# First attention of a two-block transformer: the query and key projections copied twice by ScalarE and added by GpSimd, where VectorE built them from PSUM

## The chip, the cores and the metric

The kernel runs on one core of a Trainium2 chip. The metric is the device time of one execution in microseconds (us), smaller is better. TensorE does the matrix products and writes PSUM; VectorE and ScalarE read PSUM and SBUF; GpSimd reads SBUF alone; SyncE issues the DMAs of this stage.

## The reference

The input `x` is 4 sequences of 1024 tokens with 128 features. Six sublayers follow one another, each on a normalised input and with a residual: a mixture of experts, causal attention, the same mixture again, a feed-forward layer in FP4, a second attention, the FP4 layer again. The change lies in the first attention alone:

```
def _L0_attn_ref(x, Wqkv, Wout, bout):
    qkv = x @ Wqkv.T                                # 16 heads of 8
    q, k, v = map(merge_heads, jnp.split(qkv, 3, axis=-1))
    dots = jnp.einsum('bhid,bhjd->bhij', q, k) * dh ** (-0.5)
    dots = jnp.where(causal_mask, -jnp.inf, dots)
    attn = jax.nn.softmax(dots, axis=-1)
    out = jnp.einsum('bhij,bhjd->bhid', attn, v)
    return out @ Wout.T + bout
```

## The kernel before

The first attention is one function, `attention0_stage`. The work is cut into 16 groups: 4 sequences by 4 groups of 4 heads. A head takes 32 partitions, of which 8 hold the value, 8 the part that rounding to the matmul type (`F32R`) loses, and two carry the row maximum.

Per group there are three kinds of work on the score matrix, in 20 units each (`NE` = `NM` = 20), numbered by `e`:

- MAX(e), function `max_unit`: TensorE writes scores for queries by keys (L1712, on the diagonal also L1716) into one of three PSUM buffers `pS` of 1024 columns. VectorE reduces it to maxima (L1979, `z_parts`).
- EXP(e), function `exp_unit`: TensorE writes the transposed scores, less the maximum (L1736), into a `pS` buffer. ScalarE takes the exponential into `Pr` (L1894). GpSimd zeroes what lies behind the diagonal in 8 blocks a group (`select`, L2083).
- `values` (L1750): TensorE multiplies `Pr` with V into `pO`, after several EXP units; ScalarE copies the result to `oT` (L1881).

While group G has its EXP units, group G+1 has its MAX units, and group G+2 its projections. TensorE's program in `main(G)` goes through e = 0 to 19, and at each e does MAX(G+1, e), then whatever falls due at this e (turns, a projection, `values`), then EXP(G, e). The three `pS` buffers go round over this order, so MAX(e) takes the buffer of EXP(e-2), and EXP(e) that of MAX(e-1):

```
                    if u >= 3:
                        before, g, k = USES[u - 3]
                        need(pe, *((maxed, NM * g + k + 1) if before == MAXIMUM else (exp_done, NE * g + k + 1)))
```

That is, MAX(e) on TensorE waits until ScalarE is done with the exponential of EXP(e-2), and EXP(e) waits until VectorE is done with the reduction of MAX(e-1).

A group's queries and keys come in four projections (`project`, L1662, three matmuls of 512 columns each), at e = 3, 9, 13 and 17 (`AT_PROJECT`), in the order query low half, key low half, key high half, query high half. All write one PSUM bank, `pX`, which also serves the turning of maxima (`turn_maximum`, at e = 2 and 15) and of outputs (`turn_output`, at e = 5 and 11). A projection is kept in two steps. ScalarE, ahead of its exponential of the same e, writes the rounded value to `high` (`keep_high`, L1871); VectorE, ahead of its reduction of the next e, multiplies `high` with a column of factors (0, 1 or -1 by row), adds the projection from PSUM, and writes `Q` or `QK` (`split`, L1968). `split_done` counts the latter. TensorE waits for it before it writes `pX` again and before the group's MAX(0); SyncE waits for it before it copies keys into `KM` (`spread_keys`, L1605), after which, in its queue, come the maxima into `QM` (`spread_maxima`, L1623), and queries (`spread_queries`, L1616).

There are such projections within `main` for groups 2 to 15, that is in `main(0)` to `main(13)`: 56 of them in 14 groups. The first eight are done ahead of it. `main(14)` has MAX and EXP units but no projections, `main(15)` only EXP units.

Of the kernel before, what the change touches and what calls it, by code (L numbers as in the profile page):

```python
# [4 lines left out]
F32 = mybir.dt.float32  # L5
# [5 lines left out]
P = 128  # L11
# [56 lines left out]
def need(engine, sem, n):  # L68

    if not isinstance(n, int) or n > 0:  # L70
        engine.wait_ge(sem, n)
# [1412 lines left out]
def attention0_stage(nc, C, name, Wt):  # L1484
# [9 lines left out]
    with Scope(nc, name) as s:  # L1494
# [10 lines left out]
        QK = [s.sb(f"QK{u}", [P, SEQ0], F32R) for u in range(RING)]  # L1505
        KM = [s.sb(f"KM{u}", [P, 2, SEQ0], F32R) for u in range(2)]
        QM = [s.sb(f"QM{u}", [P, 2, SEQ0 // 2], F32R) for u in range(2)]
        high = s.sb("high", [P, 512], F32R)
        Pr = [s.sb(f"Pr{u}", [P, 4, 512]) for u in range(4)]
        parts, m = s.sb("parts", [P, KT, KT, 4]), s.sb("m", [P, KT, 4])  # L1510
        mw = s.sb("mw", [P, KT, 4, 32], F32R)
# [82 lines left out]
        with nc.Block() as block:  # L1594
# [58 lines left out]
            def _(pe):  # L1653
# [112 lines left out]
                def main(G):  # L1766
                    more, further, first = G + 1 < NG, G + 2 < NG, G % 4 == 0 and G > 0
                    for e in range(NE):
                        if more:
                            max_unit(G + 1, e)  # L1770
                        if e == AT_M1:
                            need(pe, split_done, min(4 * (G + 2), 4 * NG))
                            need(pe, m_kept, 2 * G + 1)
                            turn_maximum(G, 1)
                        if e == AT_PROJECT[0] and further:
                            need(pe, m_kept, 2 * G + 2)
                            project(G + 2, Q_LOW)
                        if e == AT_O1 and G > 0:
                            need(pe, *((split_done, 4 * (G + 2) + 1) if further else (m_kept, 2 * G + 2)))
                            turn_output(G - 1, 1)  # L1780
                        if e in AT_FIN and first:
                            need(pe, o_normed, 2 * G)
                            need(pe, fin_kept, 2 * (G // 4 - 1) + AT_FIN.index(e))
                            turn_batch(G // 4 - 1, AT_FIN.index(e))
                        if e == AT_PROJECT[1] and further:
                            need(pe, split_done, 4 * (G + 2) + 1)
                            need(pe, o_normed, 2 * G)
                            if first:
                                need(pe, fin_kept, 2 * (G // 4))
                            project(G + 2, K_LOW)  # L1790
                        if e == AT_O0:
                            if further:
                                need(pe, split_done, 4 * (G + 2) + 2)
                            else:
                                need(pe, o_normed, 2 * G)
                            turn_output(G, 0)
                        if e == AT_PROJECT[2] and further:
                            need(pe, o_normed, 2 * G + 1)
                            project(G + 2, K_HIGH)
                        if e == AT_M0 and more:  # L1800
                            if further:
                                need(pe, split_done, 4 * (G + 2) + 3)
                            else:
                                need(pe, o_normed, 2 * G + 1)
                            turn_maximum(G + 1, 0)
                        if e == AT_PROJECT[3] and further:
                            need(pe, m_kept, 2 * G + 3)
                            project(G + 2, Q_HIGH)
                        for j in range(NJ):
                            if AT_V[j] == e:  # L1810
                                values(G, j)
                            if AT_V[j] - NE == e and G > 0:
                                values(G - 1, j)
                        exp_unit(G, e)
# [49 lines left out]
            def _(act):  # L1864
                a = nc.scalar

                def keep_high(G, i, k):

                    need(act, proj_done, 4 * G + k + 1)
                    need(act, split_done, 4 * G + k)  # L1870
                    a.activation(high[:, :], bank(G, i), ACT.Identity, bias=rows[:, 1 - i // 2:2 - i // 2]).then_inc(high_done, 1)  # L1871

                def keep_maximum(G, half):
                    need(act, m_turned, 2 * G + half + 1)
                    need(act, q_masked[half], 128 * G)
                    a.activation(mT[half][:, :], pX[:, :], ACT.Copy).then_inc(m_kept, 1)
# [20 lines left out]
                def main(G):  # L1897
                    more, further, first = G + 1 < NG, G + 2 < NG, G % 4 == 0 and G > 0
                    for e in range(NE):
                        if e == AT_M1:  # L1900
                            keep_maximum(G, 1)
                        if e == AT_TAKE[1] and G > 0:
                            keep_output(G - 1, 1)
                        if e == AT_TAKE[0]:
                            keep_output(G, 0)
                        if e in AT_FIN and first:
                            keep_batch(G // 4 - 1, AT_FIN.index(e))
                        if e == AT_M0 and more:
                            keep_maximum(G + 1, 0)
                        if e in AT_PROJECT and further:  # L1910
                            keep_high(G + 2, ORDER[AT_PROJECT.index(e)], AT_PROJECT.index(e))
                        exponentials(G, e)

                def high_rows(w):
# [41 lines left out]
            def _(dve):  # L1956
                v = nc.vector

                def split(G, i, k):

                    need(dve, high_done, 4 * G + k + 1)

                    dst = Q[G % 2] if i // 2 else QK[G % RING]
                    if i // 2:
                        need(dve, st_ready, NE * (G - 2) + (NE0 if i % 2 else 0) + 1 if G >= 2 else 0)
                    else:
                        need(dve, st_ready, NE * (G - RING + 1))
                    v.scalar_tensor_tensor(dst[:, (i % 2) * 512:(i % 2) * 512 + 512], high[:, :].bitcast(F32),  # L1968
                                           rows[:, 3 - i // 2:4 - i // 2], bank(G, i), ALU.mult, ALU.add).then_inc(split_done, 1)
# [34 lines left out]
                                    r.unsqueeze(3).to_broadcast([P, 4, 4, DH0]), ALU.mult).then_inc(o_normed, 1)  # L2004

                def main(G):
                    more, further = G + 1 < NG, G + 2 < NG
                    for n in range(NM + 1):
                        if n == AT_MAX and more:
                            maximum(G + 1, 0)  # L2010
                        if n == AT_O1 + 1 and G > 0:
                            output(G - 1, 1)
                        for k in range(4):
                            if n == AT_PROJECT[k] + 1 and further:
                                split(G + 2, ORDER[k], k)
                        if n == AT_O0 + 1:
                            output(G, 0)
                        if n < NM and more:
                            max_unit(G + 1, n)
                    if more:  # L2020
                        maximum(G + 1, 1)
# [52 lines left out]
            @block.gpsimd  # L2074
            def _(pool):
                g_ = nc.gpsimd

                def select(G, j, c):

                    need(pool, exp_done, NE * G + FIRST_OF[j] + 1)  # L2080
                    blk = Pr[j % 4][:, :, c * P:(c + 1) * P]

                    g_.affine_select(blk, blk, [[0, 4], [1, P]], ALU.is_ge, 0.0, base=0, channel_multiplier=-1).then_inc(selected, 1)  # L2083

                g_.memset(KM[0][:, 0, :].bitcast(F32), 0.0).then_inc(zeroed, 1)

                pool.wait_ge(xn_ready, NT)
                g_.memset(parts[:, :, :, :], -BIG).then_inc(ready, 1)
                g_.memset(V[:, :, :, DH0:DH0 + 1], 1.0).then_inc(ones_set, 1)
                g_.memset(mw[:, :, :, :].bitcast(F32), 0.0).then_inc(ready, 1)  # L2090
                for buf in (QM[0], KM[1], QM[1]):
                    g_.memset(buf[:, :, :].bitcast(F32), 0.0).then_inc(zeroed, 1)
                xt = X[:, :].rearrange("p (t f) -> p t f", f=D)
                pool.wait_ge(bo_loaded, 16)
                pool.wait_ge(xn_ready, NT)
                g_.tensor_tensor(xt, xt, bo.unsqueeze(1).to_broadcast([P, NT, D]), ALU.add).then_inc(biased, 1)
                for G in range(NG):
                    for c in range(4):
                        select(G, c, c)
                    for c in range(4):  # L2100
                        select(G, 8 + c, c)


def build(nc, d, out):
# [110 lines left out]
```

## Time and profile before

| | |
|---|---|
| median of 3 runs | 1815.1 us (1807.4 to 1815.26) |
| profiled execution, its own time | 1809.93 us |
| its span | 1808.0 us |
| stretch of this attention's groups | about 345 to 845 us |
| granted TensorE clock, mean | 0.922 |

The profile's page gives busy time by engine and the costliest groups of instructions. The trace behind it is asked for stretches: a timeline row is a start, a duration, an engine, a line of the kernel, the tensors (written <- read) and a count where like instructions ran on end; a bracket gives the idle time ahead of it on its engine and whose work ended it.

### The profile page before, as it was taken

The numbers are of one execution on the slowest core, as the hardware profiler recorded it, in microseconds if no ns is written. First come the engines' busy times: TensorE is split into PE (matmuls) and PEld (weight loads), VectorE is DVE, ScalarE is ACT, GpSimd is POOL, SyncE is SP. The second block draws the span as 40 slices with busy tenths as digits, with TensorE's granted clock in tenths as the row PEclk, the third lists the DMA queues.
The fourth block names the chain that finished last, engine by engine and source line by source line (L and its number), as shares of the span: only waits on it lengthen the run. The fifth ranks groups of instructions, "written<-read, shape, count | busy, mean of one in ns | idle before, by whom it ended". The sixth has DMA issues, their size and how long they took to land. (4 is left out here: it accounts for less than half of the span.)

```text
span 1808.0 us, 35347 instructions
## 1 busy us (share of the span) xinstructions
PE 1524.2 (84%) x12511; PEld 1008.8 (56%) x12511; DVE 1199.7 (66%) x2260; ACT 971.2 (54%) x1727; POOL 690.6 (38%) x1145
## 2 busy tenths in 40 slices
PE   6999966999999999998799896456888889888874
PEld 5568853544443444434666785234666667676653
DVE  6635558588888888883754565656566777766434
ACT  3324432377777777775343442323677667667641
POOL 0687743011111111111088764342244454453432
PEclk9999988599999999998699998677999999999987
DMA  7122521011111111110513242100000000000000
GB/s 257 35 78 75 148 84 32 20 35 27 27 39 27 36 30 34 27 26 7 208 42 92 85 131 79 52 0 1 2 2 2 5 8 5 5 8 9 7 4 13
DMA packets 49469, 81.52 MB, mean 45 GB/s; under 512 B 10868, under 2 KB 34868, under 8 KB 48628
## 3 DMA queue, kind: packets, MB, share of 16 engines
q1 hardware_dynamic: 40212, 60.50, 11.5%
q0 software_dynamic: 9088, 18.76, 3.1%
q8 instruction: 107, 1.75, 0.4%
q14 instruction: 62, 0.51, 0.1%
HBM read 43.18 MB, written 31.22 MB: 41 GB/s over the span
## 5 line engine op out<-in xcount | busy, mean ns | idle before, releaser
L1979 DVE TENSOR_REDUCE z_parts<-z_pS 128x8 f32<-128x1024 f32 (+1 forms) x320 | 350.5, 1115 | 51.4 <-PE z_pS L1712 33.4
L1894 ACT ACTIVATE z_Pr<-z_pS 128x1024 f32<-128x1024 f32 (+1 forms) x320 | 297.5, 940 | 121.2 <-PE z_pS L1736 120.6
L2083 POOL TENSOR_SCALAR_AFFINE_SELECT z_Pr<-z_Pr 128x512 f32<-128x512 f32 x128 | 80.8, 637 | 445.5 <-ACT z_Pr L1894 445.5
L356 POOL DMA_INDIRECT slot_results<-m_yq,m_xq x156 | 153.9, 987 | 75.6 <-ACT m_yq L561 45.3
L332 POOL DMA_INDIRECT slot_rows<-m_XN,m_dest x128 | 129.9, 1015 | 93.7 <-DVE m_dest L650 58.3
L1750 PE MATMUL z_pO<-z_Pr,z_V 128*9 128x512 f32 (+3 forms) x1536 | 160.2, 489 | 3.1 <-ACT z_oT L1881 1.6
L1736 PE MATMUL z_pS<-z_QM,z_QK 64*128 64x512 f32 (+1 forms) x640 | 150.4, 470 | 1.4 <-DVE z_parts L1979 0.2
L1736 PEld LDWEIGHTS z_pS<-z_QM,z_QK 64*128 64x128 f32 x640 | 59.7, 185 | 155.4 <-issue 111.6
L1712 PE MATMUL z_pS<-z_KM,z_Q 64*128 64x512 f32 (+1 forms) x640 | 133.2, 414 | 15.1 <-ACT z_Pr L1894 14.7
L974 PE MATMUL f_gup<-s_wguT,f_xT 128*128 128x352 f32 x234 | 97.7, 501 | 34.2 <-DVE f_src L1281 19.0
L705 DVE TENSOR_TENSOR m_h<-m_sg,m_gu 128x512 f32<-128x512 f32 x78 | 53.7, 688 | 90.9 <-ACT m_sg L553 90.8
L1156 ACT ACTIVATE f_vb<-f_p 64x256 f32<-64x256 f32 x256 | 97.0, 379 | 31.0 <-PE f_p L949 28.2
L1281 DVE TENSOR_TENSOR f_src<-f_sg,f_gup 128x176 f32<-128x176 f32 x117 | 38.4, 328 | 104.9 <-ACT f_sg L1125 104.3
L553 ACT ACTIVATE m_sg<-m_gu 128x512 f32<-128x512 f32 x78 | 46.6, 598 | 101.5 <-PE m_gu L450 101.5
L1125 ACT ACTIVATE f_sg<-f_gup 128x176 f32<-128x176 f32 x117 | 37.6, 321 | 107.1 <-PE f_gup L974 106.7
L1712 PEld LDWEIGHTS z_pS<-z_KM,z_Q 64*128 64x128 f32 x640 | 62.4, 191 | 40.5 <-ACT z_Pr L1894 28.2
L597 DVE TENSOR_TENSOR m_h<-m_sg,m_gu 128x512 f32<-128x512 f32 x64 | 44.0, 687 | 60.7 <-PE m_gu L374 54.2
L1444 POOL TENSOR_TENSOR f_pm<-f_Pn,k_mask 128x512 f32<-128x512 f32 x64 | 82.7, 1307 | 1.3 <-DVE f_Pn L1316 1.3
L1420 POOL TENSOR_TENSOR f_q<-f_y,f_neg 128x256 f32<-128x256 f32 x32 | 19.9, 623 | 163.6 <-issue 161.8
L1412 POOL TENSOR_SCALAR f_neg<-f_sc 128x60 f32<-128x60 f32 (+2 forms) x36 | 12.7, 353 | 181.2 <-DVE f_sc L1260 166.0
L529 ACT ACTIVATE m_sg<-m_gu 128x512 f32<-128x512 f32 x64 | 38.1, 599 | 78.0 <-PE m_gu L370 76.1
L450 PE MATMUL m_gu<-s_wh,m_xqh 128*128 x156 | 71.1, 456 | 8.4 <-issue 6.4
(296 smaller groups left out, 3852.3 us busy)
## 6 DMA issues: line engine op xcount, KB each, us to landing
slot_rows<-in_c_pad SPq DMA_DIRECT2D x2, 5070.0 KB, 24.9
m_xq<-slot_rows SPq DMA_DIRECT2D x38, 260.0 KB, 4.3
z_KM<-z_QK SPq DMA_DIRECT2D x60, 128.0 KB, 2.4
z_QM<-z_Q SPq DMA_DIRECT2D x128, 48.0 KB
m_raw<-in_gu SPq DMA_DIRECT2D x2, 2048.0 KB, 9.1
m_XN<-slot_results SPq DMA_DIRECT2D x8, 512.0 KB, 4.1
m_raw<-slot_results SPq DMA_DIRECT2D x8, 512.0 KB, 5.5
slot_results<-m_yq,m_xq POOLq DMA_INDIRECT x156
```

The source lines that it names most:

```text
L332: g_.indirect_dma_start(xs_dram, bass.IndirectOffsetOnAxis(dest[:, k, t:t + 1], 0), XN[:, t, 2 - XO[k]:2 - XO[k] + ROW], None).then_inc(se ...
L356: g_.indirect_dma_start(y_dram, bass.IndirectOffsetOnAxis(xq[q % RING][:, j % QT, TAG[list_of(j)]:TAG[list_of(j)] + 1].bitcast(I32), 0), y ...
L450: last = mm(gu[r % 2][:, u, :], xv[q % 2][:, c], wt[:, bass.ds(es[u] * GU, GU)], start=a, stop=b)
L974: mm(bank[:, 0:INNER], xT[:, j * P:(j + 1) * P], wguT[:, c, :, :].rearrange("p a k -> p (a k)"), start=True, stop=True).then_inc(gated, 1)
L1156: last = a_.activation(vb[j % 2][a * 64:(a + 1) * 64, g * 256:(g + 1) * 256].rearrange("p (k d) -> p k d", k=4), heads, ACT.Copy)
L1444: g_.tensor_tensor(pm[j % 2][:, :, :, :], Pn[:, h0:h0 + 8, :].unsqueeze(3).to_broadcast([P, 8, SEQ1, PER]), mask16[:, :].unsqueeze(1).unsq ...
L1712: last = mm(b[:, 2 * pair:2 * pair + 2, 0:width * P], Q[G % 2][r, qt * P:(qt + 1) * P], KM[G % 2][r, :, kb * P:(kb + width) * P], start=Tr ...
L1736: last = mm(b[:, 2 * pair:2 * pair + 2, 0:width * P], QK[G % RING][r, kt * P:(kt + 1) * P], QM[half][r, :, q * P:(q + width) * P], start=T ...
L1750: last = mm(pO[32 * h:32 * h + DH0 + 1, lo:512], V[:, (G // 4) * KT + kt, 4 * (G % 4) + h, :], Pr[j % 4][:, h, lo:512], start=(kt == 0), s ...
L1894: a.activation(Pr[j % 4][:, :, q * P:(q + width) * P], heads(G, EXPONENTIAL, e)[:, :, 0:width * P], ACT.Exp, scale=DH0 ** -0.5).then_inc(e ...
L1979: v.tensor_reduce(parts[:, qt, kb:kb + width, :].rearrange("p t h -> p h t"), b.rearrange("p h (t k) -> p h t k", k=P), AX.X, ALU.max).the ...
L2083: g_.affine_select(blk, blk, [[0, 4], [1, P]], ALU.is_ge, 0.0, base=0, channel_multiplier=-1).then_inc(selected, 1)
```

## The change

ScalarE's `keep_high` of the 56 projections in `main` becomes `keep_both`: `high` is now the rounded value of the projection times the factor plus the bias, both from columns of `rows`, and a second instruction copies the projection unrounded to a new SBUF tile `whole`. GpSimd adds the two into `Q` or `QK`. VectorE no longer does it. TensorE's waits before it writes `pX` again ask for `high_done`, which both copies together raise once, in place of `split_done`. GpSimd's program now has the adds between its selects, in the order of e. The first eight projections stay as they were.

```diff
-        high = s.sb("high", [P, 512], F32R)
+        high, whole = s.sb("high", [P, 512], F32R), s.sb("whole", [P, 512])
...
                         if e == AT_M1:
-                            need(pe, split_done, min(4 * (G + 2), 4 * NG))
+                            need(pe, high_done, min(4 * (G + 2), 4 * NG))
...
                         if e == AT_O1 and G > 0:
-                            need(pe, *((split_done, 4 * (G + 2) + 1) if further else (m_kept, 2 * G + 2)))
+                            need(pe, *((high_done, 4 * (G + 2) + 1) if further else (m_kept, 2 * G + 2)))
...
                         if e == AT_PROJECT[1] and further:
-                            need(pe, split_done, 4 * (G + 2) + 1)
+                            need(pe, high_done, 4 * (G + 2) + 1)
...
                         if e == AT_O0:
                             if further:
-                                need(pe, split_done, 4 * (G + 2) + 2)
+                                need(pe, high_done, 4 * (G + 2) + 2)
...
                         if e == AT_M0 and more:
                             if further:
-                                need(pe, split_done, 4 * (G + 2) + 3)
+                                need(pe, high_done, 4 * (G + 2) + 3)
...
+                def keep_both(G, i, k):
+
+                    need(act, proj_done, 4 * G + k + 1)
+                    need(act, split_done, 4 * G + k)
+                    a.activation(high[:, :], pX[:, :], ACT.Identity, bias=rows[:, 1 - i // 2:2 - i // 2], scale=rows[:, 3 - i // 2:4 - i // 2])
+                    a.activation(whole[:, :], pX[:, :], ACT.Copy).then_inc(high_done, 1)
...
                         if e in AT_PROJECT and further:
-                            keep_high(G + 2, ORDER[AT_PROJECT.index(e)], AT_PROJECT.index(e))
+                            keep_both(G + 2, ORDER[AT_PROJECT.index(e)], AT_PROJECT.index(e))
                         exponentials(G, e)
...
-                        for k in range(4):
-                            if n == AT_PROJECT[k] + 1 and further:
-                                split(G + 2, ORDER[k], k)
...
+                def split(G, i, k):
+
+
+                    pool.wait_ge(high_done, 4 * G + k + 1)
+                    need(pool, st_ready, NE * (G - 2) + (NE0 if i % 2 else 0) + 1 if i // 2 else NE * (G - RING + 1))
+                    dst = Q[G % 2] if i // 2 else QK[G % RING]
+                    g_.tensor_tensor(dst[:, (i % 2) * 512:(i % 2) * 512 + 512], high[:, :].bitcast(F32), whole[:, :], ALU.add).then_inc(split_done, 1)
...
-                    for c in range(4):
-                        select(G, c, c)
-                    for c in range(4):
-                        select(G, 8 + c, c)
+                    for e in range(NE):
+                        if e in AT_PROJECT and G + 2 < NG:
+                            split(G + 2, ORDER[AT_PROJECT.index(e)], AT_PROJECT.index(e))
+                        j = EU[e][0]
+                        if e == FIRST_OF[j] and not 4 <= j < 8:
+                            select(G, j, j % 4)
```

ScalarE, `main(1)`, e = 1 to 4, around the projection at e = 3. Before:

```order
L1894 ACTIVATE z_Pr0<-z_pS1 128x4x256
L1876 ACTIVATE z_mT1<-z_pX 128x512
L1894 ACTIVATE z_Pr1<-z_pS0 128x4x128
L1881 ACTIVATE z_oT<-z_pO 128x512
L1871 ACTIVATE z_high<-z_pX,k_rows 128x512
L1894 ACTIVATE z_Pr1<-z_pS2 128x4x256
L1894 ACTIVATE z_Pr2<-z_pS1 128x4x256
```

The same place of the changed kernel (its lines have other numbers from here on; L1901 are the exponentials):

```order
L1901 ACTIVATE z_Pr0<-z_pS1 128x4x256
L1883 ACTIVATE z_mT1<-z_pX 128x512
L1901 ACTIVATE z_Pr1<-z_pS0 128x4x128
L1888 ACTIVATE z_oT<-z_pO 128x512
L1877 ACTIVATE z_high<-z_pX,k_rows 128x512
L1878 ACTIVATE z_whole<-z_pX 128x512
L1901 ACTIVATE z_Pr1<-z_pS2 128x4x256
L1901 ACTIVATE z_Pr2<-z_pS1 128x4x256
```

One copy more stands between the rounded value and the exponential of e = 3; it is so at each of the four projections.

VectorE, the same stretch of `main(1)`, reductions of MAX(3) to MAX(5), then the output of the group before. Before:

```order
L1979 TENSOR_REDUCE z_parts<-z_pS1 128x4
L1968 SCALAR_TENSOR_TENSOR z_Q1<-z_high,k_rows,z_pX 128x512
L1979 TENSOR_REDUCE z_parts<-z_pS0 128x4x2
L1979 TENSOR_REDUCE z_parts<-z_pS2 128x4x2
L1998 RECIPROCAL z_rec<-z_pX 128x16
L2003 TENSOR_TENSOR z_at<-z_pX,z_rec 128x4x32
```

Changed:

```order
L1986 TENSOR_REDUCE z_parts<-z_pS1 128x4
L1986 TENSOR_REDUCE z_parts<-z_pS0 128x4x2
L1986 TENSOR_REDUCE z_parts<-z_pS2 128x4x2
L2005 RECIPROCAL z_rec<-z_pX 128x16
L2010 TENSOR_TENSOR z_at<-z_pX,z_rec 128x4x32
```

The one instruction on `high` is gone, nothing else moved.

GpSimd, one group of the changed kernel, where before eight selects stood on end (the adds are L2095; x2 are those of e = 9 and 13):

```order
L2087 AFFINE_SELECT z_Pr0<-z_Pr0 128x4x128
L2087 AFFINE_SELECT z_Pr1<-z_Pr1 128x4x128
L2095 TENSOR_TENSOR z_Q1<-z_high,z_whole 128x512
L2087 AFFINE_SELECT z_Pr2<-z_Pr2 128x4x128
L2087 AFFINE_SELECT z_Pr3<-z_Pr3 128x4x128
L2095 TENSOR_TENSOR z_QK0<-z_high,z_whole 128x512 x2
L2087 AFFINE_SELECT z_Pr0<-z_Pr0 128x4x128
L2087 AFFINE_SELECT z_Pr1<-z_Pr1 128x4x128
L2095 TENSOR_TENSOR z_Q1<-z_high,z_whole 128x512
L2087 AFFINE_SELECT z_Pr2<-z_Pr2 128x4x128
L2087 AFFINE_SELECT z_Pr3<-z_Pr3 128x4x128
```

TensorE's and SyncE's instructions keep their order; only the semaphores that TensorE waits on before it writes `pX` change.

## Rows read from the trace of the kernel before

**Rows 1.** The page: busy time, share and instructions of each engine.

```profile
PE 1524.2 (84%) x12511; PEld 1008.8 (56%) x12511; DVE 1199.7 (66%) x2260; ACT 971.2 (54%) x1727; POOL 690.6 (38%) x1145
```

**Rows 2.** Busy time in 31 us of the groups: PE, PEld, DVE, ACT, POOL, clock, DMA.

```profile
562.00:593.00 31.00, 29.93 (x224) 12.71 (x220) 26.35 (x35) 22.42 (x29) 5.05 (x8) 1.00 0.13 31
```

**Rows 3.** Timeline of ScalarE over one group: start, duration, instruction, idle time before.

```profile
571.69 0.59 ACT L1876 ACTIVATE z_mT<-z_pX 128x512 fp32r<-128x512 f32 x1
...
573.97 1.93 ACT L1894 ACTIVATE z_Pr<-z_pS 128x1024 f32<-128x1024 f32 x2
...
582.57 0.59 ACT L1881 ACTIVATE z_oT<-z_pO 128x512 f32<-128x512 f32 x1
583.04 0.69 ACT L1871 ACTIVATE z_high<-z_pX,k_rows 128x512 fp32r<-128x512 f32 x1
583.61 1.04 ACT L1894 ACTIVATE z_Pr<-z_pS 128x1024 f32<-128x1024 f32 x1
...
589.77 1.02 ACT L1894 ACTIVATE z_Pr<-z_pS 128x1024 f32<-128x1024 f32 x1
...
592.18 0.59 ACT L1876 ACTIVATE z_mT<-z_pX 128x512 fp32r<-128x512 f32 x1
...
595.30 0.69 ACT L1871 ACTIVATE z_high<-z_pX,k_rows 128x512 fp32r<-128x512 f32 x1 [0.52 <-PE z_pX L1662]
595.88 1.02 ACT L1894 ACTIVATE z_Pr<-z_pS 128x1024 f32<-128x1024 f32 x1
597.37 1.61 ACT L1894 ACTIVATE z_Pr<-z_pS 128x1024 f32<-128x1024 f32 x2 [0.47 <-PE z_pS L1736]
...
602.94 0.59 ACT L1876 ACTIVATE z_mT<-z_pX 128x512 fp32r<-128x512 f32 x1
```

**Rows 4.** Timeline of TensorE's matmuls in the same group.

```profile
573.84 0.40 PE L1736 MATMUL z_pS<-z_QM,z_QK 64*128 64x512 f32 x2
575.04 0.50 PE L1712 MATMUL z_pS<-z_KM,z_Q 64*128 64x512 f32 x2 [0.80 <-ACT z_Pr L1894]
...
584.70 0.50 PE L1712 MATMUL z_pS<-z_KM,z_Q 64*128 64x512 f32 x2
...
591.06 0.28 PE L1712 MATMUL z_pS<-z_KM,z_Q 64*128 64x256 f32 x2
...
597.16 0.39 PE L1712 MATMUL z_pS<-z_KM,z_Q 64*128 64x512 f32 x2
...
597.96 0.38 PE L1736 MATMUL z_pS<-z_QM,z_QK 64*128 64x256 f32 x2
598.53 0.39 PE L1712 MATMUL z_pS<-z_KM,z_Q 64*128 64x256 f32 x2 [0.20 <-ACT z_Pr L1894]
```

**Rows 5.** VectorE: the splits of the 28 query halves, by form; then its timeline.

```profile
L1968 DVE SCALAR_TENSOR_TENSOR z_Q<-z_high,k_rows,z_pX 128x512 fp32r<-128x512 f32 x28 | 20.9, 748 | 16.2 <-ACT z_high L1871 14.9 <-PE z_pS L1736 1.3
```

```profile
596.68 2.46 DVE L1979 TENSOR_REDUCE z_parts<-z_pS 128x8 f32<-128x1024 f32 x2
```

**Rows 6.** ScalarE's two copies of turned maxima in `main(14)`, which has no projections.

```profile
792.15 0.59 ACT L1876 ACTIVATE z_mT<-z_pX 128x512 fp32r<-128x512 f32 x1
811.55 0.59 ACT L1876 ACTIVATE z_mT<-z_pX 128x512 fp32r<-128x512 f32 x1
```

**Rows 7.** Groups by form: ScalarE's copies, one with a bias column; a GpSimd tensor_tensor.

```profile
L1871 ACT ACTIVATE z_high<-z_pX,k_rows 128x512 fp32r<-128x512 f32 x56 | 38.6, 689 | 10.7 <-PE z_pX L1662 8.7
L1876 ACT ACTIVATE z_mT<-z_pX 128x512 fp32r<-128x512 f32 x30 | 17.8, 593 | 0.8 <-PE z_pX L1724 0.8
L1431 POOL TENSOR_TENSOR f_wl<-f_raw,f_wh 128x512 fp32r<-128x512 f32 x2 | 2.5, 1269 | 0.0
```

**Rows 8.** GpSimd's selects of e = 18 and 19; SyncE's four key copies.

```profile
598.46 1.23 POOL L2083 TENSOR_SCALAR_AFFINE_SELECT z_Pr<-z_Pr 128x512 f32<-128x512 f32 x2 [2.98 <-ACT z_Pr L1894]
```

```profile
590.68 4.05 SPq L1605 DMA_DIRECT2D z_KM<-z_QK  x4
```

```profile
z_KM<-z_QK SPq DMA_DIRECT2D x60, 128.0 KB, 2.4
```

More of the change, by code:

```diff
@@ L2006, in main @@
                 def main(G):
-                    more, further = G + 1 < NG, G + 2 < NG
+                    more = G + 1 < NG
                     for n in range(NM + 1):
```

## Prediction

> **What bounds the kernel now.** The page comes first: TensorE is busy 84% of the span, VectorE 66%, ScalarE 54%, GpSimd 38% [rows 1]. These are averages over six sublayers, and the change touches one, so the second view is the stretch in which its groups run. There the core repeats itself: in 31 us TensorE is busy 29.93, VectorE 26.35, ScalarE 22.42 and GpSimd 5.05, with the clock granted in full [rows 2]. ScalarE's copy of a turned maximum at e = 2 comes at 571.69 and again at 602.94, so a group takes 31.25 us [rows 3]. By busy time TensorE is the limit, VectorE second, ScalarE third. But busy shares don't tell what a change on the second or third is worth; for that one must see which waits TensorE has, since its program is in order and goes on end between them.
>
> The third view is TensorE's timeline over one group, read for matmuls that start right when another engine's work ends. Five places matter:
>
> - MAX(5) at 575.04, with 0.80 us idle ahead of it [rows 4]. MAX(5) needs the exponential of EXP(3); ScalarE's two exponentials from 573.97 took 1.93 in all, one alone takes 1.02, so that of EXP(3) ended at 574.99, 0.05 ahead of the matmul [rows 3, 4].
> - MAX(11) at 584.70. The exponential of EXP(9), 583.61 plus 1.04, ended at 584.65, again 0.05 ahead [rows 3, 4]. There is no idle time ahead of it in the row, but no reserve either.
> - MAX(15) at 591.06. The exponential of EXP(13) ended at 590.79: a reserve of 0.27 [rows 3, 4].
> - MAX(19) at 597.16. That of EXP(17) ended at 596.90: a reserve of 0.26 [rows 3, 4].
> - EXP(19) at 597.96 and the next group's MAX(0) at 598.53. EXP(19) needs the reduction of MAX(18), which ended at about 596.68 plus 1.23, 597.91; this is the one place of the group where VectorE holds TensorE. I estimate the hold at 0.15 us: from MAX(19) to EXP(19) are 0.80 us, and MAX(19) with its diagonal, two rows of matmuls, accounts for some 0.65 of them. MAX(0) needs the exponential of EXP(18), 597.37 plus 1.02, 598.39 [rows 3 to 5].
>
> So MAX(5), MAX(11), MAX(15) and MAX(19) each wait, or nearly so, for the exponential that stands right behind a projection's copy in ScalarE's program. That makes ScalarE's order at the four projections, not VectorE's load, what the change acts upon.
>
> **VectorE's part, removed.** 56 splits of 0.748 us go, 3.0 us in each of 14 groups, and with them the wait ahead of each for `high`, 14.9 over the 28 query halves, 0.53 each [rows 5]: 5.1 us a group or 72 us in all. On the path only the 0.15 us at EXP(19) answers to it, 2.1 us over 14 groups, and the wait for ScalarE at the next MAX(0) right behind would take even this. I credit 0.
>
> **ScalarE's part, added.** The second copy has the shape of the copy of maxima, 0.593 [rows 7]. What counts is how far it pushes the next start: from `oT` at 582.57 (0.59 long) to `high` at 583.04 is 0.47, so such instructions overlap, and I take 0.48 [rows 3]. `high` now has a column as factor besides the column as bias. With the bias alone it is 0.689 against 0.593 without, so a column costs 0.096 [rows 7]; for the factor no row here reads PSUM with both, so it lies between 0 and 0.10, and I take 0.09, by the nearest row. Together 0.57 us a projection.
>
> The Trainium skill, in "ScalarE: Activation LUTs", section "What ACT_TABLE_LOAD costs", says that each per-partition pointer operand adds about 93 ns, factor and bias alike. The row for the bias agrees (96 ns); by the page as an estimate the sum stays as it is, by a free factor it would be 4 us less.
>
> Where does 0.57 go?
>
> - e = 3: the exponential of EXP(3) already holds MAX(5). All of it is lost: 0.57.
> - e = 9: MAX(11) has no reserve: 0.57.
> - e = 13: the exponential ends at 591.36, plus 0.05 is 591.41 against 591.06: 0.35.
> - e = 17: MAX(19) moves to 597.52, 0.36 late, EXP(19) behind it to about 598.25. But MAX(0) can't start before the exponential of EXP(18), whose matmuls lie ahead of MAX(19) and haven't moved, and which ScalarE, free at 595.88 + 0.57 + 0.91 = 597.36, can start at 597.37 as before. MAX(0) stays at 598.53: 0.
>
> Between these points TensorE goes on end, so what is lost at one isn't won back at the next. Sum: 1.49 us a group, times 14 is 20.9 us. Bounds: with a free factor 0.48 + 0.48 + 0.26 is 1.22, or 17 us; with nothing absorbed at e = 17 and 0.1 us more at the two new waits for restarting the matmul stream it is about 2.05, or 29 us.
>
> **GpSimd's part, added.** 56 adds of 128x512 fp32 into fp32r. A tensor_tensor of just this form takes 1.269 [rows 7]. GpSimd idles 26 of 31 us [rows 2], so the load, 5.1 us a group, is covered. Three users wait behind it. The selects: at e = 17 `high` starts at 595.30, both copies end at about 596.56, the add at 597.9; the next select came at 598.46, bound by its exponential [rows 3, 8]: 0.5 us to spare. The next group's MAX(0) needs all four adds: 597.9 against 598.53 [rows 4], 0.6 to spare. SyncE's key copies started at 590.68, right behind the split; the add of e = 13 ends 1.1 us later, at 591.8. They took 4.05 here to be issued and 2.4 to land [rows 8], so 598.3, just ahead of MAX(0), which itself moves by the 1.49. All at 0. If this cover were gone, each 0.1 us would cost 1.4 us in all.
>
> **TensorE's waits for `pX`** now end with ScalarE's two copies and not with the split. No turn waits for them now, so nothing is won.
>
> **Sum.** 1809.9 + 20.9 = 1830.8 us for an execution like the profiled one. This one lies 5.2 us under the median of the three runs, 1815.1; put on the median the sum is 1836.0. I forecast 1833, between the two.
>
> **Rivals.**
>
> *VectorE sets the pace after all* (faster). For it: 85% busy here, and 72 us taken from it. `main(14)` shows the most that can come: without projections it needs 811.55 - 792.15 = 19.40 us from e = 2 to e = 15, where the normal group needs 592.18 - 571.69 = 20.49 [rows 3, 6]. Three projections gone from all engines give 1.09, four some 1.45, over 14 groups 20 us. If half of this came through VectorE and ScalarE's copy cost nothing: 1800 us. It decides if TensorE waited for reductions by over 0.65 us a group more than for exponentials; I find 0.15. Chance 0.12.
>
> *ScalarE's second copy is hidden* (same). ScalarE idles 8.6 us of 31. It would need the exponentials behind projections not to be what MAX waits for; at MAX(5) and MAX(11) the 0.05 us gaps say they are. 1810 to 1815 us. Chance 0.10.
>
> *The add comes too late* (slower still). If GpSimd needs over 1.9 us from copy to result at e = 17, or the key copies land late, the next MAX(0) waits. At 2.5 us it is 0.6 a group more, 8 us: 1841. The measured 1.269 speaks against it. The Trainium skill, in "GPSIMD Engine Reference", section "Performance versus the Vector engine", puts a two-input add at 1.96 times VectorE's time. On the split's 0.748 that is an estimate of 1.47 us, still inside the 1.9; the row is shorter. Chance 0.13.
>
> *The forecast*, 0.65, own range 1825 to 1844.
>
> **How the numbers follow.** The range 1811 to 1846 takes the forecast's cases, most of the late add and the upper part of the hidden copy; the faster case and the tails are left out, some 0.2. Half a percent, 9 us, is about what a measurement of this kernel can tell from no change. Faster: 0.12. Same: the hidden copy and the forecast's lowest tail, 0.12. Slower: 0.76.
>
> **What would show it.** The period between copies of turned maxima at 32.7 us in place of 31.25; MAX(5) again right behind the exponential of EXP(3), with 1.4 us idle ahead of it in place of 0.80; MAX(11) with a wait of 0.6; VectorE's idle time up by 3 us a group and more; `high` at 0.78 us, `whole` at 0.59, the add at 1.27 with no one behind it. A period under 31.25 would prove me wrong on VectorE, one over 33.3 on the add or the keys.

## The result and the profile after

| | before | changed |
|---|---|---|
| median of 6 runs | 1807.94 us (1802.26 to 1815.26) | 1827.24 us (1819.34 to 1832.1) |
| span of the profiled execution | 1808.0 us | 1823.5 us |
| period of a group | 31.25 us | 32.75 us |

The changed kernel takes 1.0100 times the time before, 95% interval 1.0068 to 1.0132: 19.3 us slower by the medians, where 20.9 was forecast. The median before came down by 7 us with three more runs, so the absolute 1833 was some 6 us too high; the difference is what the sum was about.

The view by form over the groups (count | busy us, mean ns | idle us before and its releasers) shows the instructions that the change is made of; their counterparts in the kernel before stand in [rows 5] and [rows 7].

```profile
L1877 ACT ACTIVATE z_high<-z_pX,k_rows 128x512 fp32r<-128x512 f32 x56 | 43.6, 779 | 10.9 <-PE z_pX L1662 8.8
L2095 POOL TENSOR_TENSOR z_QK<-z_high,z_whole 128x512 fp32r<-128x512 f32 x28 | 35.7, 1274 | 155.3 <-ACT z_whole L1878 155.3
L2095 POOL TENSOR_TENSOR z_Q<-z_high,z_whole 128x512 fp32r<-128x512 f32 x28 | 35.6, 1271 | 33.9 <-ACT z_whole L1878 33.9
L1878 ACT ACTIVATE z_whole<-z_pX 128x512 f32<-128x512 f32 x56 | 33.1, 591 | 0.0
```

`high` went from 689 to 779 ns with the factor column, `whole` takes 591, the add 1271 to 1274. Busy times in 33 us of the groups (PE, PEld, DVE, ACT, POOL), against [rows 2] in 31:

```profile
445.00:478.00 33.00, 30.77 (x224) 12.82 (x222) 24.43 (x31) 25.02 (x33) 10.38 (x13) 1.00 0.13 30
```

TensorE has 2.2 us idle in 33 where it had 1.1 in 31. ScalarE's timeline of one group, as in [rows 3]:

```profile
443.58 0.59 ACT L1883 ACTIVATE z_mT<-z_pX 128x512 fp32r<-128x512 f32 x1
...
445.28 0.78 ACT L1877 ACTIVATE z_high<-z_pX,k_rows 128x512 fp32r<-128x512 f32 x1
445.96 0.59 ACT L1878 ACTIVATE z_whole<-z_pX 128x512 f32<-128x512 f32 x1
446.44 1.94 ACT L1901 ACTIVATE z_Pr<-z_pS 128x1024 f32<-128x1024 f32 x2
...
476.36 0.59 ACT L1883 ACTIVATE z_mT<-z_pX 128x512 fp32r<-128x512 f32 x1
```

And TensorE's, as in [rows 4]:

```profile
447.51 0.50 PE L1712 MATMUL z_pS<-z_KM,z_Q 64*128 64x512 f32 x2 [1.38 <-ACT z_Pr L1901]
...
457.76 0.50 PE L1712 MATMUL z_pS<-z_KM,z_Q 64*128 64x512 f32 x2 [0.48 <-ACT z_Pr L1901]
...
464.50 0.38 PE L1712 MATMUL z_pS<-z_KM,z_Q 64*128 64x256 f32 x2 [0.17 <-ACT z_Pr L1901]
...
470.95 0.49 PE L1712 MATMUL z_pS<-z_KM,z_Q 64*128 64x512 f32 x2 [0.20 <-ACT z_Pr L1901]
...
471.96 0.38 PE L1712 MATMUL z_pS<-z_KM,z_Q 64*128 64x256 f32 x2
```

The reader should see the new brackets: MAX(5) waits 1.38 us where it waited 0.80, and MAX(11), MAX(15) and MAX(19), which had no bracket, have one. Counted from the group's first copy of turned maxima (571.69 before, 443.58 now), the five matmuls stand as follows:

| | before | now | later by | added here |
|---|---|---|---|---|
| MAX(5) | 3.35 | 3.93 | 0.58 | 0.58 |
| MAX(11) | 13.01 | 14.18 | 1.17 | 0.59 |
| MAX(15) | 19.37 | 20.92 | 1.55 | 0.38 |
| MAX(19) | 25.47 | 27.37 | 1.90 | 0.35 |
| next MAX(0) | 26.84 | 28.38 | 1.54 | -0.36 |

The forecast had 0.57, 0.57, 0.35, 0.36 and back to 1.49.

VectorE, for its part, gained idle time and nothing else. Its reductions in the stretch of the groups, wider form, in the views of the kernel before and of the changed one:

```profile
L1979 DVE TENSOR_REDUCE z_parts<-z_pS 128x8 f32<-128x1024 f32 x242 | 291.9, 1222 | 31.5 <-PE z_pS L1712 22.7 <-PE z_pS L1716 8.4
L1986 DVE TENSOR_REDUCE z_parts<-z_pS 128x8 f32<-128x1024 f32 x239 | 291.1, 1224 | 101.0 <-PE z_pS L1716 55.8 <-PE z_pS L1712 45.0
```

VectorE now waits 101 us for TensorE ahead of these reductions, where it waited 31.5 us.

### The profile page after: what moved, and what is told of

It reads as the page before. It is cut to its first block and busy times, and to the rows that moved or that the text cites. A ratio compares the mean times of both kernels' runs of the same rounds, so it can differ in the third digit from the quotient of the medians.

```text
span 1823.5 us, 35401 instructions
## 1 busy us (share of the span) xinstructions
PE 1520.8 (83%) x12509; PEld 1003.3 (55%) x12511; DVE 1165.5 (64%) x2204; ACT 999.5 (55%) x1783; POOL 759.5 (42%) x1201
## 5 line engine op out<-in xcount | busy, mean ns | idle before, releaser
L1901 ACT ACTIVATE z_Pr<-z_pS 128x1024 f32<-128x1024 f32 (+1 forms) x320 | 293.4, 942 | 109.9 <-PE z_pS L1736 109.5
L2095 POOL TENSOR_TENSOR z_QK<-z_high,z_whole 128x512 fp32r<-128x512 f32 x28 | 35.7, 1274 | 155.3 <-ACT z_whole L1878 155.3
```

The costliest lines, as they stand in the source:

```text
L1901: a.activation(Pr[j % 4][:, :, q * P:(q + width) * P], heads(G, EXPONENTIAL, e)[:, :, 0:width * P], ACT.Exp, scale=DH0 ** -0.5).then_inc(e ...
```

## The experiments

The experiments ran on three chips, each kernel beside the kernel before on the same chip, with 5 to 12 executions of a kernel and 16 to 30 of the kernel before. These chips ran the kernel before at 1838 to 1844 us, where it took 1808 above, so only ratios and the period of a group are compared. The period is the distance from one group's copy of turned maxima to the next group's, in the profiled execution. Groups 4, 8 and 12 also turn a sequence's result and take longer, most by 0.85 us; all periods given are those of the others. The kernel before has one profile, with the period 31.25; the changed kernel has two, on two chips, with the same period in both.

| kernel | period, us | time against before (95%) |
|---|---|---|
| before | 31.25 | 1 |
| changed | 32.76 | 1.0100 (1.0068 to 1.0132) |
| changed, on another chip | 32.76 | 1.0100 (1.0069 to 1.0131) |
| no second copy | 31.45 | 1.0028 (1.0001 to 1.0054) |
| before, plus a copy | 32.57 | 1.0109 (1.0085 to 1.0132) |
| double add | 33.43 | 1.0149 (1.0116 to 1.0183) |
| three copies | 34.70, some 36.25 | 1.0304 (1.0281 to 1.0327) |
| copy behind the exponential | 31.42 | 1.0025 (1.0005 to 1.0044) |
| both copies of e = 9 behind | 32.40 | 1.0070 (1.0045 to 1.0095) |
| changed, reordered | 30.81 | 0.9940 (0.9918 to 0.9962) |
| before, reordered | 31.82 | 1.0043 (1.0021 to 1.0066) |
| changed, reordered at e = 17 too | 30.56 | 0.9948 (0.9923 to 0.9973) |

My theory was that of the prediction: the loss is the time by which ScalarE's copies push back the exponential behind them, at the places where TensorE waits for it, and VectorE's relief is worth nothing. The rivals: GpSimd's adds or the later key copies are the loss; VectorE's relief is worth something and the copies cost more; ScalarE's total load counts, not its order.

**The second copy taken out.**

```diff
-                    a.activation(high[:, :], pX[:, :], ACT.Identity, bias=..., scale=...)
-                    a.activation(whole[:, :], pX[:, :], ACT.Copy).then_inc(high_done, 1)
+                    a.activation(high[:, :], pX[:, :], ACT.Identity, bias=..., scale=...).then_inc(high_done, 1)
...
+                g_.memset(whole[:, :], 0.0)
```

> The changed kernel without ScalarE's second copy: whole is set to zero once and GpSimd adds the constant, so the queries and keys of groups 2 to 15 lack their unrounded part and the output is not the reference's. VectorE still has no splits, GpSimd still has its adds. My theory (the copy ahead of the exponential is the whole loss, VectorE's relief is worth nothing): only the factor column of high is left, 0.09 us at e = 3 and at e = 9, swallowed at e = 13 and 17. Period 31.4 us against 31.25 before, time 2 to 3 us above the kernel before. Rival (VectorE's relief is worth something that the copy hides): a period clearly under 31.25, down to 30, and a time 5 to 15 us under the kernel before.

This kernel leaves out the unrounded part. The period is 31.45. Of the 1.51 us, 1.31 are gone with this one instruction, while the adds and the missing splits are still there. (The adds and the keys do come one copy earlier; whether they matter, the next two experiments test.) What is left, 0.20, is two times the 0.09 of the factor column, and no relief by VectorE shows. The time is 1.0028 of the kernel before, by the interval just above it.

**The kernel before with a copy added.**

```diff
                         if e in AT_PROJECT and further:
                             keep_high(G + 2, ORDER[AT_PROJECT.index(e)], AT_PROJECT.index(e))
+                            a.activation(whole[:, :], wh[:, 0:512].bitcast(F32), ACT.Copy)
                         exponentials(G, e)
```

> The kernel before, with one ScalarE copy more behind keep_high at each of the 56 projections (from SBUF into a tile that nobody reads). VectorE keeps its splits, nothing goes to GpSimd. My theory: 0.48 us at e = 3 and e = 9, 0.2 at e = 13, none at e = 17, so a period of 32.4 and 16 to 18 us above the kernel before, 3 to 5 below the changed one. Rival (the loss of the change is in GpSimd's adds or the later key copies): within 3 us of the kernel before. Rival (VectorE's relief did help in the changed kernel): clearly slower than the changed kernel.

```profile
L1912 ACT ACTIVATE z_whole<-s_wh 128x512 f32<-128x512 f32 x49 | 30.6, 625 | 0.0
```

That is the view by form of this kernel. With VectorE's splits in place and nothing on GpSimd the period is 32.57, 1.32 above before, so the copy alone makes nearly the whole loss. That is 0.17 above the 1.15 expected. The copy from SBUF takes 625 ns where the one from PSUM takes 591, and this difference is paid at three places, 0.10 in all; the rest is the 0.05 us from the exponential's end to MAX(15), which the 0.2 expected at e = 13 had left out. The changed kernel has 0.19 more. At e = 3, 9 and 13 its factor column pushes 0.09 and its copy 0.03 less than this one, 3 times 0.06 together, so the splits that it no longer has on VectorE were worth less than these views resolve. By time I had expected this kernel 3 to 5 us below the changed one; the two can't be told apart (1.0109 and 1.0100, intervals that overlap widely).

**Each add done twice.**

```diff
+                    g_.tensor_tensor(spare[:, :], high[:, :].bitcast(F32), whole[:, :], ALU.add)
                     g_.tensor_tensor(dst[:, (i % 2) * 512:(i % 2) * 512 + 512], high[:, :].bitcast(F32), whole[:, :], ALU.add).then_inc(split_done, 1)
```

> The changed kernel with each GpSimd add done twice, first into a spare tile: 2.5 us from copy to result in place of 1.27. My theory: the add was covered by 0.6 us only at e = 17; with the doubled one the next group's MAX(0) waits for it some 0.7 us, the key copies still land in time. Period about 33.4 us, 8 to 11 us above the changed kernel. Rival (the add was already on the path): 1.27 us a group or more, 18 us or more above. Rival (wide cover): nothing.

TensorE's weight loads of this kernel show the next group's MAX(0) behind GpSimd:

```profile
430.67 0.18 PEld L1713 LDWEIGHTS z_pS<-z_KM,z_Q 64*128 64x128 f32 x2 [0.73 <-POOL z_Q L2097]
...
464.10 0.19 PEld L1713 LDWEIGHTS z_pS<-z_KM,z_Q 64*128 64x128 f32 x2 [0.73 <-POOL z_Q L2097]
```

The period is 33.43, 0.67 above the changed kernel: of 1.27 us more a projection, 0.6 were covered, as worked out. The list of this kernel's waits names no DMA, so the keys, which come later by as much, held nothing up. The add is not on the path of the changed kernel, but more than 0.6 us of further work on GpSimd at e = 17 would put it there.

**A third copy.**

```diff
+                    a.activation(spare[:, :], pX[:, :], ACT.Copy)
                     a.activation(whole[:, :], pX[:, :], ACT.Copy).then_inc(high_done, 1)
```

> The changed kernel with a third ScalarE copy of each projection, into a spare tile, between high and whole. My theory: now there is no reserve left anywhere, so 0.48 us is lost at all four projections: period 32.75 + 1.9 = 34.7 us, 25 to 28 us above the changed kernel. Rival (the copies are partly hidden in ScalarE's idle time): 10 us or less.

Seven of the thirteen periods behind the first group are undisturbed and 34.7 (or 35.6 with a turned sequence), 1.94 above the changed kernel: with the reserves gone, all four places pay 0.48. That is as expected. But the time rose by 0.0204 of 1841, some 38 us, and not 27. Six periods are 1.55 us longer than their like, 9.3 us in all, and a table by stretches shows what goes with it. Its columns are the stretch, its length, the busy time of PE, PEld, DVE, ACT and POOL, then the granted clock, the DMA share and GB/s. First such a group, with MAX(5) at 408.93, then one without, with MAX(5) at 445.18:

```profile
404.00:409.00 5.00, 3.14 (x29) 1.82 (x28) 2.97 (x3) 4.95 (x9) 1.59 (x2) 1.00 0.08 18
409.00:410.00 1.00, 1.00 (x8) 0.69 (x8) 0.21 (x1) 0.79 (x1) 0.45 (x2) 1.00 0.00 0
410.00:411.00 1.00, 1.00 (x10) 0.12 (x8) 1.00 (x2) 0.00 (x0) 0.49 (x1) 0.64 0.00 0
411.00:412.00 1.00, 1.00 (x10) 0.16 (x2) 0.47 (x3) 0.00 (x0) 0.00 (x0) 0.50 0.00 0
412.00:413.00 1.00, 1.00 (x8) 0.47 (x12) 0.10 (x1) 0.53 (x1) 0.00 (x0) 0.50 0.00 0
413.00:414.00 1.00, 1.00 (x10) 0.03 (x2) 1.00 (x1) 0.06 (x1) 0.64 (x1) 0.65 0.07 18
...
440.00:445.00 5.00, 3.32 (x29) 1.99 (x27) 3.22 (x4) 4.95 (x9) 1.38 (x3) 1.00 0.05 13
445.00:446.00 1.00, 0.82 (x6) 0.56 (x7) 0.00 (x0) 1.00 (x2) 0.56 (x1) 1.00 0.00 0
446.00:447.00 1.00, 1.00 (x13) 0.32 (x10) 0.96 (x1) 0.04 (x1) 0.63 (x1) 1.00 0.06 16
```

In the first the granted clock was 0.50 of full from 411 to 413 and between the two in the slices on either side. Eight matmuls of `values`, 1.04 us long in the other group, took 1.79 there:

```profile
408.93 0.50 PE L1713 MATMUL z_pS<-z_KM,z_Q 64*128 64x512 f32 x2 [1.86 <-ACT z_Pr L1903]
...
410.12 1.79 PE L1751 MATMUL z_pO<-z_Pr,z_V 128*9 128x512 f32 x8
```

**The copy moved behind the exponential.** At e = 3, 9 and 13:

```diff
                     a.activation(high[:, :], pX[:, :], ACT.Identity, bias=..., scale=...)
+                    if e is not None:
+                        exponentials(G - 2, e)
                     a.activation(whole[:, :], pX[:, :], ACT.Copy).then_inc(high_done, 1)
...
-                            keep_both(G + 2, ORDER[AT_PROJECT.index(e)], AT_PROJECT.index(e))
-                        exponentials(G, e)
+                            keep_both(G + 2, ORDER[AT_PROJECT.index(e)], AT_PROJECT.index(e), e if e in (3, 9, 13) else None)
+                        if not (further and e in (3, 9, 13)):
+                            exponentials(G, e)
```

> The changed kernel, but at e = 3, 9 and 13 the copy to whole stands behind the exponential of the same e and not ahead of it; high stays ahead, e = 17 is as in the changed kernel. All the same instructions run. My theory: the exponentials that MAX(5), MAX(11) and MAX(15) wait for come 0.48 us earlier again, only the factor column's 0.09 us is lost at e = 3 and 9; the exponentials of e = 4, 10 and 14, now later, have that much reserve. Period 31.4 to 31.5 us, 2 to 5 us above the kernel before. Rival (ScalarE's total load is what costs): a period of 32.5 or more, as in the changed kernel.

```profile
402.38 0.78 ACT L1877 ACTIVATE z_high<-z_pX,k_rows 128x512 fp32r<-128x512 f32 x1
403.06 1.01 ACT L1903 ACTIVATE z_Pr<-z_pS 128x1024 f32<-128x1024 f32 x1
403.96 0.60 ACT L1880 ACTIVATE z_whole<-z_pX 128x512 f32<-128x512 f32 x1
404.44 1.03 ACT L1903 ACTIVATE z_Pr<-z_pS 128x1024 f32<-128x1024 f32 x1
```

The same instructions on the same engines, three pairs of them swapped, and the period is 31.42 where it was 32.76. ScalarE's load is not what costs; the place in its queue is. This is the plainest of the experiments.

**Both copies of e = 9 behind the exponential.**

```diff
-                        if e in AT_PROJECT and further:
+                        if e in AT_PROJECT and e != 9 and further:
                             keep_both(G + 2, ORDER[AT_PROJECT.index(e)], AT_PROJECT.index(e))
                         exponentials(G, e)
+                        if e == 9 and further:
+                            keep_both(G + 2, ORDER[AT_PROJECT.index(e)], AT_PROJECT.index(e))
```

> The changed kernel with both copies of the projection of e = 9 behind the exponential of EXP(9). My theory: MAX(11) waits no more, 0.57 us of the 1.5 come back and nothing else changes: period 32.2 us, 12 to 14 us above the kernel before. Rival (a loss at one place is made up at the next, so that repairing one doesn't help): period 32.6 or more.

The period is 32.40: 0.36 came back, not 0.57. The view of weight loads names what took the rest, the turn of outputs at e = 11, which writes `pX` and must now wait until ScalarE has read it:

```profile
416.25 0.42 PEld L1757 LDWEIGHTS z_pX<-k_ident,z_oT 128*128 128x128 f32 x4 [0.36 <-ACT z_whole L1878]
```

What I had not counted is that a copy moved back on ScalarE also frees `pX` later. Counted from the start of the projection's last matmul, `whole` ends at 3.04 us here and at 1.98 in the changed kernel. Where `whole` alone was moved, it ended at 2.89; TensorE came to the turn at 3.01 and did not wait.

**A new order for the changed kernel.** If order is what costs, order may also win back the 0.80 us that MAX(5) waited in the kernel before. TensorE does the projections of e = 3 and 9 behind EXP(e), so that the exponential need not wait for the projection; the turn of outputs at e = 5 goes behind `values`; EXP(18) goes ahead of `values`. ScalarE keeps to it.

```diff
@@ main of TensorE
-                        if e == AT_PROJECT[0] and further:
-                            need(pe, m_kept, 2 * G + 2)
-                            project(G + 2, Q_LOW)
-                        if e == AT_O1 and G > 0:
...
-                            turn_output(G - 1, 1)
...
-                        if e == AT_PROJECT[1] and further:
...
-                            project(G + 2, K_LOW)
...
+                        if e == 18:
+                            exp_unit(G, e)
                         for j in range(NJ):
                             if AT_V[j] == e:
                                 values(G, j)
...
-                        exp_unit(G, e)
+                        if e == AT_O1 and G > 0:
...
+                            turn_output(G - 1, 1)
+                        if e != 18:
+                            exp_unit(G, e)
+                        if e == AT_PROJECT[0] and further:
...
+                            project(G + 2, Q_LOW)
+                        if e == AT_PROJECT[1] and further:
...
+                            project(G + 2, K_LOW)
@@ main of ScalarE
+                        if e in (3, 9) and further:
+                            exponentials(G, e)
                         if e in AT_PROJECT and further:
-                            keep_both(G + 2, ORDER[AT_PROJECT.index(e)], AT_PROJECT.index(e))
-                        exponentials(G, e)
+                            keep_both(G + 2, ORDER[AT_PROJECT.index(e)], AT_PROJECT.index(e), e if e in (13,) else None)
+                        if not (further and e in (3, 9, 13)):
+                            exponentials(G, e)
```

> The changed kernel with another order around the projections: TensorE does the projections of e = 3 and 9 behind EXP(e), the turn of outputs at e = 5 behind values, and EXP(18) ahead of values; ScalarE keeps the projections of e = 3 and 9 behind the exponential, that of e = 13 with the exponential between its two copies. My theory: the 0.8 us that MAX(5) waited in the kernel before is gone, and some 0.4 of the wait at the next MAX(0); VectorE, without splits, keeps up. Period 29.9 to 30.3 us, 13 to 19 us under the kernel before. Rival (TensorE then waits for VectorE or the adds instead): 31 us or more, no gain.

MAX(19), the first line, has a bracket now, and MAX(5) of the next group has none:

```profile
427.32 0.50 PE L1712 MATMUL z_pS<-z_KM,z_Q 64*128 64x512 f32 x2 [0.36 <-ACT z_Pr L1906]
...
435.50 0.40 PE L1712 MATMUL z_pS<-z_KM,z_Q 64*128 64x512 f32 x2
```

The period is 30.81 and the time 0.9940 of the kernel before, 0.9918 to 0.9962: 11 us under it and some 29 under the changed kernel. That is less than I expected (29.9 to 30.3, and 13 to 19 us under). Counted from the group's first copy of turned maxima, MAX(5) stands 0.57 earlier than in the kernel before, but MAX(19) only 0.06: TensorE comes to it earlier, and waits 0.36 for the exponential of EXP(17), which still stands behind two copies. I had followed the gain at MAX(0) and not the wait just ahead of it.

**The same order for the kernel before.**

> The kernel before with the same new order on TensorE and with keep_high of e = 3 and 9 behind the exponential; VectorE still does the splits. My theory: here VectorE's splits do matter, since high comes 0.7 to 0.9 us later and VectorE, in order, waits for it ahead of the reductions that EXP(5) and EXP(11) need. Some 0.35 won at e = 3, up to 0.7 lost at e = 9, some 0.4 won at MAX(0): period 31 to 31.5 us, within 5 us of the kernel before. Rival (the order alone is the gain, VectorE's splits are nowhere on the path): as fast as the reordered changed kernel, 30 us.

Its diff on TensorE is the same with `split_done` for `high_done`; ScalarE does `keep_high` of e = 3 and 9 behind the exponential.

```profile
411.77 0.75 DVE L1973 SCALAR_TENSOR_TENSOR z_QK<-z_high,k_rows,z_pX 128x512 fp32r<-128x512 f32 x1 [1.58 <-ACT z_high L1874]
412.43 2.35 DVE L1984 TENSOR_REDUCE z_parts<-z_pS 128x8 f32<-128x1024 f32 x2
```

```profile
408.19 0.50 PE L1736 MATMUL z_pS<-z_QM,z_QK 64*128 64x512 f32 x2 [0.59 <-DVE z_parts L1984]
...
413.71 0.50 PE L1736 MATMUL z_pS<-z_QM,z_QK 64*128 64x512 f32 x2 [0.48 <-DVE z_parts L1984]
```

VectorE stands 1.58 us in its queue for `high` of e = 9, two reductions come late, and TensorE waits 0.48 ahead of EXP(11) for the first. It is the same behind e = 3, where I had expected a gain: VectorE waits 1.49 us for `high`, and TensorE later 0.16 ahead of EXP(7) and 0.59 ahead of EXP(8). The period is 31.82, longer than before and than the 31 to 31.5 expected, where the changed kernel in this order has 30.81; by time it is 8 us above the kernel before, not within 5. Here VectorE's splits are on the path, and the whole change, ScalarE's second copy included, wins 1.0 us a group. So the relief that was worth nothing in the order of before is what makes the better order pay.

**And e = 17.** The last run puts the projection of e = 17 behind EXP(17) and its copies behind the exponential.

> The reordered changed kernel with the projection of e = 17, too, behind EXP(17) on TensorE and behind the exponential on ScalarE. My theory: MAX(19), which still waited 0.4 us for the exponential of EXP(17), waits no more; the add of the query high half comes out level with the next MAX(0) and takes a part back. Period 30.5 us against 30.8, 3 to 5 us under the reordered kernel without it. Rival (the add, now the last to come, takes all of it back): 30.8 or more.

```profile
421.96 0.49 PE L1712 MATMUL z_pS<-z_KM,z_Q 64*128 64x512 f32 x2
...
423.12 0.19 PEld L1712 LDWEIGHTS z_pS<-z_KM,z_Q 64*128 64x128 f32 x2 [0.23 <-POOL z_Q L2103]
```

MAX(19) waits no more, MAX(0) is now released by the add, and the period is 30.56 as expected. By time, 0.9948, it can't be told from the version before it (0.9940, on another chip); 14 groups of 0.25 us are 3.5 us, less than the interval.

> The changed kernel itself once more, on the chip of the reordered one, as a common measure. Period 32.75 us, 1.0 to 1.2% above the kernel before.

It came out so: 32.76 us and 1.0100.

## Why the prediction was right

*What bounds the kernel.* Right. The four exponentials behind projections are what TensorE waits for. The swap of `whole` and the exponential shows it: order alone takes back 1.34 of 1.51 us.

*VectorE's part at nothing.* Right in the order of before. Taking out the copy leaves 31.45, not a period under 31.25. In the new order it would have been wrong: there the change as a whole wins 1.0 us a group.

*ScalarE's part.* 0.57 us a projection was forecast; `high` grew by 0.090 and the exponential's start moved by 0.58 at MAX(5). The factor column at 0.09 was taken from the row of a bias column, 0.096. The Trainium skill ("ScalarE: Activation LUTs", "What ACT_TABLE_LOAD costs") gives about 93 ns for each pointer operand. This trace agrees: 689 ns with the bias column, 779 with both.

*Where it goes.* Right at each of five places to 0.03 us, the absorption at MAX(0) included. The sum was 1.49 a group, measured 1.50 to 1.53.

*GpSimd's part.* The add takes 1.27 as forecast. The estimate of 1.47 us in the prediction took the 1.96 times VectorE's time from the Trainium skill ("GPSIMD Engine Reference", "Performance versus the Vector engine"). It is too long for this shape and type: 1.271 to 1.274 is 1.70 times the split's 0.748. The measurement decides. The cover of 0.6 us at e = 17 was measured by the doubled add: 1.27 - 0.67 = 0.60.

*The sum.* 20.9 forecast, 19.3 measured by medians whose runs vary by several us. By the two traces the fourteen groups take 20.2 us more: thirteen take 1.50 to 1.53 each, and the first 0.52, from 32.66 to 33.18. The first pays the copies as well: its MAX(5) waits 0.92 us where it waited 0.27, and its MAX(11), MAX(15) and MAX(19) wait 0.47, 0.20 and 0.21 where they had no wait. But in the execution of the kernel before the granted clock was half for the first 6.3 us of this group, and in that of the changed one for the first 3.5. So the kernel before lost more of this group to the clock, which fits the 1 us that is missing. The two profiled executions as a whole differ by only 15.4 us (1809.9 and 1825.3), since the groups happened to begin 5.8 us earlier in the second, ahead of all that was changed; the stretch of the groups is the better measure. In the upper bound, the 0.1 us for restarting the matmul stream came from no row, and no run shows it: MAX(11) and MAX(15) came within 0.03 us of the forecast without it.

*What was off* is the level. I put 1833 between the profiled execution and a median of three runs; with six runs the median before is 1807.9.

## What to carry to other kernels

A busy share, or even the sum of an engine's waits, doesn't price work that is moved from one engine to another. Find the few matmuls that start right when an exponential or a reduction ends, ask what stands ahead of that instruction in its queue, and count only how far the change pushes it back, less the reserve; each place by itself, since later waits may absorb some. And if an instruction must be added to a queue, put it behind the one that the bounding engine waits for, but look who waits for the buffer that it frees.

## What the runs showed of the hardware that I had not expected

A wait can cost more than its own length. In the kernel with three copies TensorE idled 1.86 us ahead of MAX(5) in each group behind the first, and in six of the thirteen periods behind the first the granted clock then went from full (2.4 GHz) to half (1.2 GHz) about 1.4 us after it had resumed, for some 3 us, and these periods were 1.55 us longer. In the other seven the same idle time passed at full clock. With 1.38 us idle, in the changed kernel and in the one with the doubled add, the clock stayed at 1.00 through all thirteen. That this wait brings the clock down is inferred from where the falls stand, and what decides between the groups is open; no run tests either.
